# Attention 0: queries in parts of 64 with 96 keys, the transposed product, and sums of probabilities by VectorE

## The reference, cut to what matters

```python
B, T, C = x.shape                  # 8, 512, 128
H, D, window_size = (16, 64, 32)
qkv = rms_norm(x) @ w_qkv.T
q, k, v = jnp.split(qkv, 3, axis=-1)
q = apply_rope(q, cos, sin)
k = apply_rope(k, cos, sin)
attn = jnp.einsum('bhqd,bhkd->bhqk', q, k) * scale
mask = (q_pos >= k_pos) & (q_pos - k_pos <= window_size)
attn = jnp.where(mask[None, None], attn, NEG)
attn = jax.nn.softmax(attn, axis=-1)
out = jnp.einsum('bhqk,bhkd->bhqd', attn, v)
return out @ w_out.T
```

## Time and profile before

| | us |
|---|---|
| median of three runs | 1511.54 |
| lowest, highest | 1507.83, 1516.27 |
| profiled execution | 1510.9 |
| its span, first to last instruction | 1509.1 |
| PE, DVE, ACT, POOL busy | 1189.2, 831.8, 650.0, 441.5 |

### The profile page before, as it was taken

The page is one execution under the profiler, slowest core; times in us unless marked ns, Lnnn a source line. Parts: engine busy times, 40 slices in busy tenths (PEclk is TensorE's granted clock), DMA queues, the critical chain, the costliest instruction groups (busy, mean ns, idle before and its releaser), DMA issues. The chain is left out here.

```text
span 1509.1 us, 23126 instructions
## 1 busy us (share of the span) xinstructions
PE 1189.2 (79%) x7482; PEld 863.0 (57%) x7482; DVE 831.8 (55%) x1722; ACT 650.0 (43%) x2039; POOL 441.5 (29%) x255
## 2 busy tenths in 40 slices
PE   2699999999999999999751378676269999836665
PEld 1277777777777777777650245353236666624544
DVE  4275664656475664656365633102146665478985
ACT  1276564757566574756310133312025555422231
POOL 1322121312222121212100078786600000053651
PEclk9599999999999899999855679787659999967777
DMA  8212121212222121212040124345310000000000
GB/s 256 56 44 62 36 57 42 57 40 56 56 49 62 28 56 40 57 42 57 1 115 0 54 51 77 61 69 117 29 54 1 1 0 0 1 0 7 15 13 22
DMA packets 65401, 69.49 MB, mean 46 GB/s; under 512 B 13120, under 2 KB 52400, under 8 KB 65216
## 3 DMA queue, kind: packets, MB, share of 16 engines
q1 hardware_dynamic: 53216, 57.49, 15.3%
q0 software_dynamic: 11840, 10.76, 4.7%
q10 hardware_dynamic: 288, 0.53, 0.1%
HBM read 24.49 MB, written 10.70 MB: 23 GB/s over the span
## 5 line engine op out<-in xcount | busy, mean ns | idle before, releaser
L721 POOL TENSOR_TENSOR qk_cos<-qk_raw,const 128x1024 f32<-128x1024 f32 x64 | 153.6, 2400 | 471.5 <-ACT qk_raw L565 471.5
L554 ACT ACTIVATE prob<-psS,neg_max 128x160 f32<-128x160 f32 x512 | 196.7, 409 | 5.6 <-DVE neg_max L624 5.6
L624 DVE TENSOR_REDUCE neg_max<-psS 128x4 f32<-128x640 f32 x128 | 105.3, 822 | 119.8 <-PE psS L432 119.8
L518 PEld LDWEIGHTS psO<-v_tok,probT 128*128 128x128 f32 x1024 | 135.6, 194 | 47.4 <-issue 32.3
L445 PE MATMUL psQ<-a_xnT,weights 128*128 128x512 f32 x256 | 155.3, 690 | 5.4 <-ACT qk_raw L565 4.0
L518 PE MATMUL psO<-v_tok,probT 128*128 128x64 f32 x1024 | 131.5, 272 | 10.1 <-DVE o_norm L657 8.7
L565 ACT COPY qk_raw<-psQ 128x512 f32<-128x512 f32 x128 | 75.3, 589 | 136.2 <-PE psQ L445 136.1
L554 ACT ACTIVATION_READ_ACCUMULATOR prob<-psS,neg_max 128x1 f32 x512 | 113.1, 221 | 0.0
L1287 POOL DMA_INDIRECT sums<-ex_y,ex_index x64 | 102.8, 1606 | 30.5 <-issue 19.4
L432 PE MATMUL psS<-qk_roped 64*128 64x160 f32 (+1 forms) x1024 | 104.2, 324 | 0.0
L1277 POOL DMA_INDIRECT ex_rows<-rows,ex_index x64 | 66.2, 1034 | 130.0 <-issue 130.0
(11 more groups left out here) (284 smaller groups left out, 2275.4 us busy)
## 6 DMA issues: line engine op xcount, KB each, us to landing
qk_swapped<-qk_raw SPq DMA_DIRECT2D x256, 128.0 KB, 2.3
mod<-mod_rows SPq DMA_DIRECT2D x8, 512.0 KB, 7.7
ex_w<-in_L_ffn_W SPq DMA_DIRECT2D x16, 256.0 KB, 3.1
x<-in_L_attn_x POOLq DMA_DIRECT2D x4, 512.0 KB, 12.5
rows<-rt_h SPq DMA_DIRECT2D x8, 256.0 KB, 2.4
sums<-rt_zeros SPq DMA_DIRECT2D x8, 256.0 KB, 2.7
out<-x SPq DMA_DIRECT2D x8, 256.0 KB, 2.3
mod<-mod_rows SPq DMA_DIRECT2D x4, 448.0 KB, 5.1
```

The source lines that it names most:

```text
L518: ins = nc.tensor.matmul(psO[:, hd], probT[:, n, :], v[:, par, t, hd], start=(n == 0), stop=(t == 0), skip_group_check=True)
L554: last = nc.scalar.activation(prob[:, s, j, i, :], psS[:, s, j, i * KW:(i + 1) * KW], ACT.Exp, bias=nmax[:, s, 2 * j + i:2 * j + i + 1], a ...
L624: nc.vector.tensor_reduce(nmax[:, u % 2, :].rearrange("p (j i) -> p j i", j=2), psS[:, u % 2, :, 0:2 * KW].rearrange("p j (i w) -> p j i w ...
L721: nc.gpsimd.tensor_tensor(rcos[:, i, :, :], raw[:, i, :, :], cos, ALU.mult).then_inc(cos_done, 1)
```

## The change

- The scores of a tile are formed for two halves of 64 queries (a = 0, 1), each against 96 keys: its own 64 and the 32 before them. So there are eight products of 64 x 96 in place of four of 128 x 160, the mask has 192 columns in place of 320, and maxima, exponentials and sums run over 4 x 96 elements in place of 4 x 160.
- The sums are no longer accumulated by ACT with the exponentials. DVE forms them in one reduction over the unit's 384 probabilities, takes the reciprocals, and multiplies the probabilities by them (`divide`), before PE transposes them. PE's transposes of unit u wait for `normed_ready` where they waited for `exp_done`.
- The product is formed transposed: the values are the stationary operand and the probabilities the moving one, eight products of 64 x 64, straight into the layout of `oT`. `normalise`, the 32 x 32 transposes and `turn_o` go.
- The values stand in windows of 96 keys (`vw`), filled by three DMAs for each quad from `v`, which has one buffer now.

```diff
 WIN = 32
-KW = WIN + P
+HALF = P // 2
+KW = WIN + HALF
...
-    q, k = np.arange(P)[:, None], np.arange(KW)[None, :] - WIN
+    q, k = np.arange(P)[:, None] % HALF, np.arange(KW)[None, :] - WIN
     seen = (q >= k) & (q - k <= WIN)
     for first in range(2):
-        m = np.where(seen & (k >= 0) if first else seen, 0.0, NEG).astype(np.float32)
+        m = np.where(seen & ((k >= 0) | (np.arange(P)[:, None] >= HALF)) if first else seen, 0.0, NEG).astype(np.float32)
...
-        v = sb("v_tok", [P, 2, TILES, 4 * D])
+        v, vw = sb("v_tok", [P, TILES, 4 * D]), sb("v_windows", [KW, 2, 2, TILES, 4 * D])
-        probT, probTp = sb("probT", [P, 4, P]), sb("probT_prev", [P, 2, 4, WIN])
+        probT = sb("probT", [KW, 4, P])
-        o, oT = sb("o_norm", [P, 2, 4 * D]), sb("oT", [P, PAIRS, T])
+        oT = sb("oT", [P, PAIRS, T])
-        psO = ctx.enter_context(nc.psum_tensor("psO", [P, 512], F32))
-        psOT = ctx.enter_context(nc.psum_tensor("psOT", [P, 512], F32))
+        psO = ctx.enter_context(nc.psum_tensor("psO", [P, 2, 512], F32))
-        scored, turned, applied, o_turned = sem("scored"), sem("turned"), sem("applied"), sem("o_turned")
+        scored, turned, applied = sem("scored"), sem("turned"), sem("applied")
...
-                    for j in range(2):
-                        lo = 0 if t == 0 else WIN
-                        rows = slice(D * j, D * j + D)
-                        last = nc.tensor.matmul(psS[:, s, j, i * KW + WIN - lo:(i + 1) * KW],
-                                                qk[rows, par, i, 0, t * P:(t + 1) * P],
-                                                qk[rows, par, i, 1, t * P - lo:(t + 1) * P],
-                                                start=False, stop=True, skip_group_check=True)
+                    for a in range(2):
+                        lo = 0 if t == 0 and a == 0 else WIN
+                        q0 = t * P + a * HALF
+                        for j in range(2):
+                            rows = slice(D * j, D * j + D)
+                            last = nc.tensor.matmul(psS[a * HALF:(a + 1) * HALF, s, j, i * KW + WIN - lo:(i + 1) * KW],
+                                                    qk[rows, par, i, 0, q0:q0 + HALF],
+                                                    qk[rows, par, i, 1, q0 - lo:q0 + HALF],
...
-            def turn_o(b, u):
-
-                wait(pe, o_ready, b * UNITS + u + 1)
-                wait(pe, oT_ready, b * UNITS + u)
-                for i in range(2):
-                    last = nc.tensor.transpose(psOT[:, i * P:(i + 1) * P], o[:, u % 2, i * P:(i + 1) * P], k.ident)
-                last.then_inc(o_turned, 1)
...
-                    wait(pe, exp_done, b * UNITS + u + 1)
+                    wait(pe, normed_ready, b * UNITS + u + 1)
                     wait(pe, probT_ready, b * UNITS + u)
-                    for j in range(2):
-                        for i in range(2):
-                            ins = nc.tensor.transpose(psT[:, 2 * j + i, :], prob[:, u % 2, j, i, WIN:KW], k.ident)
+                    for n in range(4):
+                        ins = nc.tensor.transpose(psT[0:KW, n, :], prob[:, u % 2, n // 2, n % 2, :], k.ident)
...
                     wait(pe, probT_ready, b * UNITS + u + 1)
-                    wait(pe, o_ready, b * UNITS + u)
+                    wait(pe, oT_ready, b * UNITS + u - 1)
                     if t == 0:
-                        wait(pe, piece_out, b * QUADS * PIECES + (g + 1) * PIECES)
-                    else:
-                        wait(pe, prev_turned, b * QUADS * (TILES - 1) + g * (TILES - 1) + t)
-                    heads = [(2 * j + i, slice((2 * i + j) * D, (2 * i + j + 1) * D)) for j in range(2) for i in range(2)]
-                    for n, hd in heads:
-                        ins = nc.tensor.matmul(psO[:, hd], probT[:, n, :], v[:, par, t, hd],
-                                               start=(n == 0), stop=(t == 0), skip_group_check=True)
-                    if t > 0:
-                        for n, hd in heads:
-                            ins = nc.tensor.matmul(psO[0:WIN, hd], probTp[P - WIN:P, u % 2, n, :],
-                                                   v[P - WIN:P, par, t - 1, hd], start=False, stop=True,
-                                                   skip_group_check=True)
+                        wait(pe, v_placed, (b * QUADS + g + 1) * 48)
+                    for i in range(2):
+                        for a in range(2):
+                            for j in range(2):
+                                hd = slice((2 * i + j) * D, (2 * i + j + 1) * D)
+                                ins = nc.tensor.matmul(psO[D * j:D * j + D, u % 2, i * P + a * HALF:i * P + (a + 1) * HALF],
+                                                       vw[:, par, a, t, hd], probT[:, 2 * j + i, a * HALF:(a + 1) * HALF],
+                                                       start=True, stop=True, skip_group_check=True)
                     ins.then_inc(applied, 1)
                     for q, m in pieces[1:]:
                         project(b, q, m)
-                    if u > 0:
-                        turn_o(b, u - 1)
                     if u == 9 and not last:
...
-                turn_o(b, UNITS - 1)
...
-                if not (isinstance(b, int) and b * UNITS + u < 2):
-                    wait(act, rsum_ready, b * UNITS + u - 1)
-                    q, t = divmod(u - 2, TILES)
-                    wait(act, prev_turned, b * QUADS * (TILES - 1) + q * (TILES - 1) + t)
                 for j in range(2):
                     for i in range(2):
                         last = nc.scalar.activation(prob[:, s, j, i, :], psS[:, s, j, i * KW:(i + 1) * KW], ACT.Exp,
-                                                    bias=nmax[:, s, 2 * j + i:2 * j + i + 1],
-                                                    accum_out=psum_[:, s, 2 * j + i:2 * j + i + 1])
+                                                    bias=nmax[:, s, 2 * j + i:2 * j + i + 1])
...
-                        wait(act, applied, b * UNITS + (q - 1) * TILES)
-                    ins = nc.scalar.copy(v[:, par, 2 * (m - 4):2 * (m - 4) + 2, :],
+                    if m == 4:
+                        wait(act, v_placed, (b * QUADS + q) * 48)
+                        if not (isinstance(b, int) and b == 0 and q == 0):
+                            wait(act, applied, b * UNITS + (q - 1) * TILES)
+                    ins = nc.scalar.copy(v[:, 2 * (m - 4):2 * (m - 4) + 2, :],
                                          psQ[:, :].rearrange("p (t d) -> p t d", t=2))
...
-                wait(act, o_turned, b * UNITS + u + 1)
+                wait(act, applied, b * UNITS + u + 1)
                 nc.scalar.copy(oT[:, 2 * g:2 * g + 2, t * P:(t + 1) * P],
-                               psOT[:, 0:2 * P].rearrange("p (i q) -> p i q", i=2)).then_inc(oT_ready, 1)
+                               psO[:, u % 2, 0:2 * P].rearrange("p (i q) -> p i q", i=2)).then_inc(oT_ready, 1)
...
-            def normalise(b, u):
-
-                wait(dve, applied, b * UNITS + u + 1)
-                nc.vector.tensor_tensor(o[:, u % 2, :].rearrange("p (i j d) -> p j i d", i=2, j=2),
-                                        psO[:, 0:4 * D].rearrange("p (i j d) -> p j i d", i=2, j=2),
-                                        rsum[:, u % 2, :].rearrange("p (j i) -> p j i", j=2).unsqueeze(3).to_broadcast([P, 2, 2, D]),
-                                        ALU.mult).then_inc(o_ready, 1)
-
+            def divide(b, u):
+
+                n = b * UNITS + u + 1
+                heads = prob[:, u % 2, :, :, :].rearrange("p j i w -> p (j i) w")
+                wait(dve, exp_done, n)
+                nc.vector.tensor_reduce(psum_[:, u % 2, :], heads, AX.X, ALU.add).then_inc(sum_ready, 1)
+                wait(dve, sum_ready, n)
+                nc.vector.reciprocal(rsum[:, u % 2, :], psum_[:, u % 2, :]).then_inc(rsum_ready, 1)
+                wait(dve, rsum_ready, n)
+                nc.vector.tensor_tensor(heads, heads, rsum[:, u % 2, :].unsqueeze(2).to_broadcast([P, 4, KW]),
+                                        ALU.mult).then_inc(normed_ready, 1)
+
+            nc.vector.memset(vw[0:WIN, :, 0, 0, :], 0.0).then_inc(v_zeroed, 1)
             own.turn(0)
...
-                    wait(dve, exp_done, b * UNITS + u + 1)
-                    wait(dve, o_ready, b * UNITS + max(u - 1, 0))
-                    nc.vector.reciprocal(rsum[:, u % 2, :], psum_[:, u % 2, :]).then_inc(rsum_ready, 1)
-                    if t > 0:
-
-                        wait(dve, applied, b * UNITS + u - 1)
-                        nc.vector.transpose(probTp[P - WIN:P, u % 2, :, :],
-                                            prob[0:WIN, u % 2, :, :, 0:WIN].rearrange("p j i w -> p (j i) w")).then_inc(prev_turned, 1)
-                    if u > 0:
-                        normalise(b, u - 1)
                     roping = t < 2 and not (last and g + 1 >= QUADS)
```

(35 more changed lines are left out.)

4 lines of the change are left out of this document (2 added, 2 removed).

## The result

The changed kernel takes 1539.3 us (median of 4 runs, 1537.6 to 1542.4) against 1512.1 for the kernel before: ratio 1.018 [1.015, 1.022], or 27 us slower. The forecast had the sign but half the size: 1525, +13.5. The time went where it was looked for, in attention 0 (670.9 us in the profile before, 697.3 after, from PE's first transposes to the end of the last output projection), but mostly not by the step that I had priced.

A forecast was written before the change was run, and what follows sets the result against it. PE, over 90% busy in attention 0, was taken as the bound, its gain lost to new waits: 1510.9 - 1 + 4 + 14 (clock falls) = 1528, stated as 1525, 0.9% slower; 8-in-10 range 1490 to 1550.

The forecast's parts named there:

- POOL adds to it: Attention 0: two-tensor SBUF operations of DVE stand until POOL is done; third quad's `sines` or multiplication delayed, 1.0 us taken.
- The swaps behind them on SP's queue are needed a quad later: DMAs queued on SP behind the windows' three DMAs at the end of t = 1: not needed until a quad later.
- The clock term: Attention 0: PE's new waits lower TensorE's granted clock; +4 us at 7 sequence starts, +14 for 12 falls in quads.
- Rival 1: The clock does not fall in the quads: 1512 us, or 1504 with a loop 0.1 shorter; chance 0.27.
- The sum without the clock, -1: Attention 0: what PE gains over all sequences the waits take, together -1 us before clock falls.
- Its terms, -1.8, -1.2 and +2.5: Sequence changes: -0.3 times 6 for the repeats, -1.2 for sequence 0, +2.5 for sequence 7's last quad.
- The step from the sum's 1528 down to 1525: Terms summed to 1528; 1525 was stated because the bounds lie more to the low side.
- the loop model: Turned probabilities, ACT's copy, exponentials, DVE's sum, reciprocal, multiplication: 4.05 us before PE's next turning, was 2.8; a quad 17.6.
- The transfers of the windows: Three DMAs a quad, issued at the end of t = 1, needed two units later: 2.3 us to landing, hidden.
- the one with everything one by one (1550): Transposed product and scores run one by one, units t = 2 and 3 each 0.5 us longer: 1550; chance 0.12.
- Rival 2: PE's gain decides: product in pairs (0.56), scores by all quarters (0.45), `divide` 0.2 shorter: 1485; chance 0.15.

The follow-up runs named there:

- Run 9: Changed kernel plus twenty spare mask products behind unit 3 and units t = 0 except unit 0: 1521.5 us, ratio 1.002 to the kernel before.
- run 2: Changed kernel with POOL's second cosines of a quad waiting for DVE's first `sines`: 1513.7 us, ratio 1.000 to the kernel before.
- run 3: Changed kernel with POOL's cosine products covering 32 of 512 columns, the rest left out: 1470.8 us, 0.972 of the kernel before.
- run 1: Changed kernel with the sums back on ACT's exponentials, DVE keeping reciprocal and multiplication: 1463.4 us, ratio 0.967 to the kernel before.
- run 4: Changed kernel without sum, reciprocal and multiplication, PE's transposes waiting for the exponentials: 1443.9 us, 0.954 of the kernel before.
- run 6: Changed kernel with DVE forming each unit's sum twice, the first result unused: 1578.6 us, ratio 1.036 to the kernel before.
- run 5: Changed kernel plus twenty spare mask products behind all units t = 0 and unit 3: 1563.0 us, ratio 1.024 to the kernel before.

## Why the prediction fell short

**The step that failed is "POOL adds to it".** The mechanism stood in it: a DVE operation with two tensors from SBUF stands until POOL is done. Its place and size were wrong. I found the multiplication safe "in most units" and let a hold fall in the third quad only, on `sines` or the multiplication, for 1.0 us a sequence, 7 us in all. The trace has `sines` held in units 8 and 12 (6.1 each, forecast 5.0 and 4.0) and `h` and the multiplication in unit 3 (7.7, forecast 4.5): 1.1 + 2.1 + 3.2 = 6.4 us a sequence beyond the forecast, 45 in all. What I did not follow is how the two starts move in unit 8. `sines` waits for four DMAs that SP issues 0.6 us apart, so the last lands 3 x 0.6 + 2.3 = 4.1 us behind the first issue; before, 5.2 us of PE's unit t = 3 covered that, now only 4.0. "The swaps behind them on SP's queue are needed a quad later" was the sentence that hid it: the last ones are needed within a unit. POOL waits for no DMA; its second cosines start with the copy of the piece one unit later, 5.2 us behind the first issue before (365.62) and 4.1 now. The lines of before and after, SP's issues and then `sines`:

```profile
360.39 7.60 SPq L750 DMA_DIRECT2D qk_swapped<-qk_raw  x8
364.52 1.23 DVE L631 TENSOR_TENSOR qk_swapped<-qk_swapped,const 128x1024 f32<-128x1024 f32 x1 [0.20 <-DMA qk_swapped<-qk_raw]
...
378.08 6.43 SPq L731 DMA_DIRECT2D qk_swapped<-qk_raw  x8
382.24 3.37 DVE L616 TENSOR_TENSOR qk_swapped<-qk_swapped,const 128x1024 f32<-128x1024 f32 x1 [0.33 <-DMA qk_swapped<-qk_raw]
```

So a race that DVE won by 1.1 us (`sines` was first, and only the later `rope` was held, to 1.68) is lost by 0.1. In unit 12 the two stand alike, `sines` at 402.15 and POOL at 402.04. For unit 3, the second step of `h` was over 0.6 us ahead of POOL's start before (341.69, 342.32) and begins 0.6 behind it now (357.06, 356.42).

The Trainium skill ("SBUF — State Buffer", Who interferes with whom) says that the order of issue decides who blocks, and that a DVE instruction with two SBUF inputs contends with a GpSimd one that reads SBUF. The trace agrees: POOL first by 0.09 gives 3.37 for 1.22, DVE first by 0.24 gives POOL 3.20 for 2.36.

**The clock term was right in kind, and low in number.** Forecast: +4 for falls at all 7 starts, four of which the kernel before had too, and +14 for 12 falls of 1.2 us in the quads, that is 15 more falls and +18. Measured: 26 stretches where there were four, 22 more. Run 9 has 21 fewer than the changed kernel and gives back 25 us by the ratios (the two intervals leave some 18 to 32) and 15.6 by the profiles, 0.7 to 1.2 for each. That there are more is in part the failed step again: with waits of 3.2 us most stretches last 6.8. In run 2, with waits of 2.2 in units 8 and 12, there are still 26, but with 120 us in all. In run 3, with 1.1, there are 13, seven of them at the starts of sequences, so that without the hold six fell in the quads and not twelve. Rival 1's condition is nearest to run 9: 1514 in the scale of before, for its 1512, though not with its lengths of units.

**The sum without the clock, -1, was wrong too, though run 9 makes it look right.** (Its terms, -1.8, -1.2 and +2.5, give -0.5; the slip changes nothing.) Run 9 holds the clock about where it was before, 24 us at the lower level in both, and its ratio leaves +2.4 us [-3, +8]. But in the profiles attention 0 takes 681.7 us for 670.9, and where the clock is 1.00 on both sides a sequence takes 85.8 and 86.1 for 83.6 and 83.7. Of these 2.3 us some 0.6 are the fillers' (units 4 to 7 take 17.4, in run 3 16.8). That leaves some 1.7 a sequence, 12 us in seven, where I had -0.3 a sequence; it is an estimate from these rows. The step from the sum's 1528 down to 1525 went the wrong way, too. The 6.4 us of holds are met in part by units that are shorter than I made them: t = 1 takes 3.6 to 4.0 at full clock (forecast 4.3), t = 2 4.7 (5.0), t = 3 4.02 (4.3), some 0.8 in a quad, and by the starts of sequences, where 6.6 was 6.1. The rest I did not trace unit by unit. By this estimate the clock's share of the 27 us is some 15 and no more than the 18 that I gave it; by run 9's ratio it is 25. The runs don't settle it. Run 3 shows the plain error of the loop model: without the hold a quad takes 16.8, not 17.6.

**Its parts.** Right: the maximum, sum and multiplication at 0.56, 0.55 and 0.56, the reciprocal 0.18, the loop 4.05 (run 3: 4.06), the product 0.82 (0.84; 0.05 for each of sixteen with its load of 64 columns, between the forecast's 0.07 one by one and 0.035 in pairs), the mask 0.26 (0.28). Wrong: the turning keeps 0.44 for 0.33, the scores take 0.49 for 0.89, and a piece ahead of the product 1.06 for 0.96. The transfers of the windows took 3.6 and 4.0 us for the larger two where I had 2.3 for all, and stayed hidden as said: no wait of PE ends with them. Of the rivals, the one with everything one by one (1550) is out: sixteen scores in 0.49 are 0.03 each. Rival 2, that PE's gain decides, comes nearest to run 3, where POOL is out of the way: 0.972 x 1512 = 1470, under its 1485. But its point, a loop under 3.8, wasn't met (4.06), and the product didn't run in 0.56; the gain stands mostly at t = 3 (4.02 for 5.18).

**What stays open.** Holds and falls of the clock feed each other, so 70 us (run 3), 28 (run 2) and 16 to 25 (run 9) cannot be added, and the 27 us can't be divided between them. No run keeps the clock with the hold gone. Run 2's 28 us include less time at the lower clock (120 us for 174), run 1's 77 too (64). Runs 3, 4 and 6 are single runs, and the `issue` stops of PE where a sequence begins (1.5 to 1.9 us, in runs 5 and 9) have no cause that a profile names.

## What to carry to other kernels

Before work is moved to DVE, list which of its instructions read two tensors from SBUF and where POOL's stand in time, and ask of each pair who starts first and by how much; a margin of some tenths of a microsecond is a coin, and a faster engine elsewhere can turn even one of a whole microsecond. A wait that stands right behind a stage that is being shortened loses its cover (here a group of DMAs issued one by one), even if the transfer itself is not touched. When one filler experiment lands on a place with a cost of its own, move the filler before concluding: run 5 said that the clock is worth nothing, run 9 that it is worth some 16 to 25 us.

## What the runs showed of the hardware that I had not expected

- A held instruction ended not with the other's but most of its own length behind it: `sines` (1.22) became 3.37 and ended 1.1 behind POOL's, the multiplication (0.56) 2.33 and 0.4 behind, a step of `h` (0.69) 2.63 and 0.5 behind. Which of the two waits turned on 0.1 us.
- The sixteen scores of 64 x 96, in four quarters of the array, took 0.49 us from start to start of the next group; sixteen products with 64 columns of weights, in two halves, took 0.82.
- Turning with 96 columns of weights in place of 128 took the same 0.44 us.
- A half-clock stretch lasted 6.8 us behind most waits over 3 us, while PE was busy for 5.2 to 5.8 us of it.
